# Attention stage: row scores and maxima nearly two heads ahead of the column scores

## The reference, cut to what matters

```
_L1_attn_ref(x, W_qkv, b_qkv, W_out, b_out):      # x: (2, 1024, 512), 16 heads of 32
    q, k, v = split(x @ W_qkv.T + b_qkv)
    scores = einsum('bqhe,bkhe->bhqk', q, k) / sqrt(32)
    scores = where(causal, scores, -inf)
    attn = softmax(scores, axis=-1)
    out = einsum('bhqk,bkhe->bqhe', attn, v)
    out = out.reshape(b, l, 512) @ W_out.T + b_out
```

## Time and profile before

| | |
|---|---|
| median of 3 runs | 1735.79 us (1732.49 to 1737.97) |
| the profiled execution | 1735.57 us |
| its span, first to last instruction | 1733.7 us |
| TensorE clock granted, mean | 0.985 of full |
| busy over the span: PE / DVE / ACT / POOL | 1661.0 / 1018.7 / 655.5 / 557.8 us |
| attention stage within the span | from about 769 to 1157 us |

### The profile page before, as it was taken

The page is one execution under the profiler, slowest core; times in us unless marked ns, Lnnn a source line. Parts: engine busy times, 40 slices in busy tenths (PEclk is TensorE's granted clock), DMA queues, the critical chain, the costliest instruction groups (busy, mean ns, idle before and its releaser), DMA issues. The chain is left out here.

```text
span 1733.7 us, 21900 instructions
## 1 busy us (share of the span) xinstructions
PE 1661.0 (96%) x7804; PEld 1295.1 (75%) x7804; DVE 1018.7 (59%) x1667; ACT 655.5 (38%) x1271; POOL 557.8 (32%) x540
## 2 busy tenths in 40 slices
PE   5999999999999999999989989989999999999998
PEld 3676888788788877876656656658888888888887
DVE  4321365564623454358988989855655555555785
ACT  4421322232213332228878878762222222222221
POOL 4201210310310003117777767672144031033320
PEclk9999999999999999989999999999999999999999
DMA  7200210110101038843554545323010010012243
GB/s 287 102 12 1 61 49 19 55 31 20 60 7 37 25 108 250 291 170 75 121 120 106 122 112 133 79 73 129 0 52 25 1 49 25 1 49 71 76 133 134
DMA packets 101916, 141.80 MB, mean 82 GB/s; under 512 B 43881, under 2 KB 52713, under 8 KB 100274
## 3 DMA queue, kind: packets, MB, share of 16 engines
q1 hardware_dynamic: 100946, 134.05, 26.4%
q10 hardware_dynamic: 864, 6.39, 1.2%
HBM read 93.74 MB, written 46.53 MB: 81 GB/s over the span
## 5 line engine op out<-in xcount | busy, mean ns | idle before, releaser
L1538 ACT ACTIVATE prob<-p_turn 128x512 f32<-128x512 f32 (+3 forms) x384 | 176.2, 487 | 56.9 <-PE p_turn L1510 36.9
L1577 DVE TENSOR_TENSOR pt_lo<-prob,pt_hi 128x512 fp32r<-128x512 f32 (+3 forms) x256 | 173.7, 703 | 33.7 <-ACT pt_hi L1546 33.2
L1570 DVE TENSOR_REDUCE row_top<-p_score 128x1 fp32r<-128x128 f32 (+7 forms) x256 | 184.6, 746 | 14.4 <-PE p_score L1494 12.5
L1025 DVE TENSOR_TENSOR hid<-hid,p_up 128x512 f32<-128x512 f32 x64 | 44.0, 687 | 218.2 <-PE p_up L490 202.5
L1593 POOL TENSOR_TENSOR pt_lo<-prob,pt_hi 128x512 fp32r<-128x512 f32 (+1 forms) x128 | 167.0, 1305 | 10.7
L1924 DVE TENSOR_TENSOR e_hid<-e_hid,e_p_up 128x512 f32<-128x512 f32 x64 | 44.0, 687 | 196.4 <-PE e_p_up L1819 196.4
L1524 PE MATMUL p_o<-pt_hi,v 128*65 128x512 f32 (+3 forms) x384 | 137.9, 362 | 3.9 <-POOL pt_lo L1593 2.3
L1590 POOL TENSOR_SCALAR pt_hi<-prob 128x512 fp32r<-128x512 f32 (+1 forms) x128 | 100.9, 788 | 106.3 <-ACT prob L1538 64.2
L1525 PE MATMUL p_o<-pt_lo,v 128*65 128x512 f32 (+3 forms) x384 | 128.5, 341 | 0.0
L1546 ACT ACTIVATE pt_hi<-prob 128x512 fp32r<-128x512 f32 (+3 forms) x256 | 120.6, 486 | 3.2 <-PE p_o L1525 0.2
L772 ACT ACTIVATE hid<-p_gate 128x512 f32<-128x512 f32 x64 | 38.3, 599 | 218.7 <-PE p_gate L490 218.6
(11 more groups left out here) (279 smaller groups left out, 4256.7 us busy)
## 6 DMA issues: line engine op xcount, KB each, us to landing
stack<-qk_parked SPq DMA_DIRECT2D x66, 256.0 KB, 4.9
raw<-in_wgu SPq DMA_DIRECT2D x64, 256.0 KB, 2.7
qk_parked<-qk SPq DMA_DIRECT2D x16, 1024.0 KB, 4.0
v_parked<-v_out SPq DMA_DIRECT2D x16, 520.0 KB, 7.4
o_parked<-o_both SPq DMA_DIRECT2D x64, 128.0 KB
stack_third<-qk_parked SPq DMA_DIRECT2D x30, 256.0 KB, 4.4
v<-v_parked ACTq DMA_DIRECT2D x6, 1040.0 KB, 8.3
res<-in_x SPq DMA_DIRECT2D x8, 512.0 KB
```

Of the source, the lines that this page charges most:

```text
L1538: act.activation(prob[:, n % PB, c0:W], p_turn[:, n % TB, c0:W], ACT.Exp).then_inc(exped, 1)
L1570: dve.tensor_reduce(top[:, h % 2, r:r + 1], p_score[:, r % 2, 0:width_of(r)], AX_X, ALU.max, negate=True).then_inc(topped, 1)
L1577: dve.tensor_tensor(pt_lo[:, n % PT, c0:W], prob[:, n % PB, c0:W], pt_hi[:, n % PT, c0:W].bitcast(F32), ALU.subtract).then_inc(split, 1)
```

## The change

The lists of all engines except GpSimd are new: rows 1 to 7 are scored and reduced two heads ahead, row 0 (and, on TensorE, row 1) three heads ahead, with `AHEAD` = 3. In the iteration -1 TensorE and VectorE follow a list of their own, `FIRST`. The loads of a pair of heads are issued together at the beginning of each even head, before any place. On ScalarE round 2 moves to the next iteration's start, `read_o` of group 0 comes after exp 4, and round 5 comes after exp 6 where it came before it.

```diff
--- before.py
+++ after.py
@@ -1365,25 +1365,32 @@
     PT = 6
     K3 = 3 * E
     OS = len(o_stored)
-    AHEAD = 2
+    AHEAD = 3
     OWN = (1, 4, 6, 8)
     ORDER = {
-        "tensor": [("weigh", 0, 0), ("weigh", 1, 0), ("score", 5, 1), ("weigh", 2, 0), ("weigh", 3, 0), ("turned", 6, 0),
-                   ("score", 6, 1), ("turned", 7, 0), ("turned", 8, 0), ("weigh", 4, 0), ("weigh", 5, 0), ("score", 7, 1),
-                   ("score", 0, 2), ("turned", 9, 0), ("turned", 10, 0), ("turned", 11, 0), ("weigh", 6, 0),
-                   ("weigh", 7, 0), ("turned", 0, 1), ("score", 1, 2), ("score", 2, 2), ("turned", 1, 1),
-                   ("turned", 2, 1), ("weigh", 8, 0), ("weigh", 9, 0), ("score", 3, 2), ("weigh", 10, 0),
-                   ("weigh", 11, 0), ("score", 4, 2), ("turned", 3, 1), ("turned", 4, 1), ("turned", 5, 1)],
-        "scalar": [("exp", 3, 0), ("exp", 4, 0), ("round", 3, 0), ("exp", 5, 0), ("round", 5, 0), ("read_o", 0, 0),
-                   ("exp", 6, 0), ("exp", 7, 0), ("exp", 8, 0), ("round", 7, 0), ("exp", 9, 0), ("exp", 10, 0),
-                   ("round", 9, 0), ("exp", 11, 0), ("round", 10, 0), ("round", 11, 0), ("exp", 0, 1),
-                   ("round", 0, 1), ("exp", 1, 1), ("exp", 2, 1), ("round", 2, 1), ("read_o", 1, 0)],
-        "vector": [("top", 4, 1), ("rest", 2, 0), ("rest", 3, 0), ("top", 5, 1), ("rest", 5, 0), ("top", 6, 1),
-                   ("rest", 7, 0), ("top", 7, 1), ("top", 0, 2), ("rest", 9, 0), ("top", 1, 2), ("top", 2, 2),
-                   ("rest", 10, 0), ("rest", 11, 0), ("rest", 0, 1), ("top", 3, 2)],
+        "tensor": [("weigh", 0, 0), ("score", 2, 2), ("weigh", 1, 0), ("score", 3, 2), ("weigh", 2, 0), ("weigh", 3, 0),
+                   ("turned", 5, 0), ("turned", 6, 0), ("score", 4, 2), ("turned", 7, 0), ("score", 5, 2), ("turned", 8, 0),
+                   ("weigh", 4, 0), ("turned", 9, 0), ("score", 6, 2), ("turned", 10, 0), ("turned", 11, 0),
+                   ("weigh", 5, 0), ("score", 7, 2), ("weigh", 6, 0), ("turned", 0, 1), ("weigh", 7, 0),
+                   ("turned", 1, 1), ("score", 0, 3), ("weigh", 8, 0), ("weigh", 9, 0), ("weigh", 10, 0),
+                   ("weigh", 11, 0), ("turned", 2, 1), ("turned", 3, 1), ("score", 1, 3), ("turned", 4, 1)],
+        "scalar": [("exp", 3, 0), ("round", 2, 0), ("round", 3, 0), ("exp", 4, 0), ("read_o", 0, 0), ("exp", 5, 0),
+                   ("exp", 6, 0), ("round", 5, 0), ("exp", 7, 0), ("exp", 8, 0), ("round", 7, 0), ("exp", 9, 0),
+                   ("exp", 10, 0), ("round", 9, 0), ("exp", 11, 0), ("round", 10, 0), ("round", 11, 0), ("exp", 0, 1),
+                   ("round", 0, 1), ("exp", 1, 1), ("read_o", 1, 0), ("exp", 2, 1)],
+        "vector": [("top", 1, 2), ("rest", 2, 0), ("rest", 3, 0), ("top", 2, 2), ("top", 3, 2), ("top", 4, 2),
+                   ("top", 5, 2), ("rest", 5, 0), ("top", 6, 2), ("rest", 7, 0), ("rest", 9, 0), ("rest", 10, 0),
+                   ("rest", 11, 0), ("top", 7, 2), ("rest", 0, 1), ("top", 0, 3)],
         "gpsimd": [("divide", 4, 0), ("divide", 6, 0), ("divide", 8, 0), ("divide", 1, 1)],
-        "sync": [("place", 4, 1), ("store", 0, 0), ("place", 5, 1), ("place", 6, 1), ("place", 7, 1),
-                 ("stack", 2, 0), ("place", 0, 2), ("place", 1, 2), ("place", 2, 2), ("place", 3, 2), ("store", 1, 0)],
+        "sync": [("stack", 2, 0), ("place", 1, 2), ("store", 0, 0), ("place", 2, 2), ("place", 3, 2), ("place", 4, 2),
+                 ("place", 5, 2), ("place", 6, 2), ("place", 7, 2), ("store", 1, 0), ("place", 0, 3)],
+    }
+    FIRST = {
+        "tensor": [("score", 2, 2), ("score", 3, 2), ("score", 4, 2), ("turned", 0, 1), ("turned", 1, 1), ("score", 5, 2),
+                   ("turned", 2, 1), ("turned", 3, 1), ("score", 6, 2), ("turned", 4, 1), ("score", 7, 2),
+                   ("score", 0, 3), ("score", 1, 3)],
+        "vector": [("top", 1, 2), ("top", 2, 2), ("top", 3, 2), ("top", 4, 2), ("rest", 0, 1), ("top", 5, 2),
+                   ("top", 6, 2), ("top", 7, 2), ("top", 0, 3)],
     }
 
     with ExitStack() as ctx:
@@ -1439,9 +1446,9 @@
                 else:
                     engine.wait_ge(split, n + 1 - owned(n))
 
-        def run(steps, order):
+        def run(steps, engine):
             for h in range(-AHEAD, HB * QUADS):
-                for step, n, ahead in order:
+                for step, n, ahead in FIRST[engine] if h == -1 and engine in FIRST else ORDER[engine]:
                     if 0 <= h + ahead < HB * QUADS:
                         steps[step](h + ahead, n)
 
@@ -1451,9 +1458,9 @@
         def _(sp):
             def next_stack(h, n):
                 pair = h // 2 + n
-                if pair < HEADS:
+                if h % 2 == 0 and pair < HEADS:
                     wait(sp, turned, 2 * BL * (pair - 2))
-                    load_part(sp, slots[pair % 3], qk_dram, pair, h % 2, stacked[pair % 3])
+                    load_stack(sp, slots[pair % 3], qk_dram, pair, stacked[pair % 3])
                 if h == HB * (QUADS - 1):
                     load_next(sp)
 
@@ -1473,7 +1480,7 @@
                     .then_inc(o_stored[i], 16)
 
             sp.wait_ge(*qk_last)
-            run({"stack": next_stack, "place": place, "store": store}, ORDER["sync"])
+            run({"stack": next_stack, "place": place, "store": store}, "sync")
 
         @block.tensor
         def _(pe):
@@ -1525,7 +1532,7 @@
                 pe.matmul(p_o[0:VC, c0:W], lhs, pt_lo[:, slot, c0:W], start=False,
                           stop=(j in (QB - 1, BL - 1))).then_inc(weighted, 1)
 
-            run({"score": score, "turned": turned_score, "weigh": weigh}, ORDER["tensor"])
+            run({"score": score, "turned": turned_score, "weigh": weigh}, "tensor")
 
         @block.scalar
         def _(act):
@@ -1558,7 +1565,7 @@
 
                     load_values(act, v, v_dram, quad + 1, at // 4, v_loaded[at // 4])
 
-            run({"exp": exp, "round": round_block, "read_o": read_o}, ORDER["scalar"])
+            run({"exp": exp, "round": round_block, "read_o": read_o}, "scalar")
 
         @block.vector
         def _(dve):
@@ -1577,7 +1584,7 @@
                 dve.tensor_tensor(pt_lo[:, n % PT, c0:W], prob[:, n % PB, c0:W], pt_hi[:, n % PT, c0:W].bitcast(F32),
                                   ALU.subtract).then_inc(split, 1)
 
-            run({"top": top_row, "rest": rest}, ORDER["vector"])
+            run({"top": top_row, "rest": rest}, "vector")
 
         @block.gpsimd
         def _(pool):
@@ -1595,7 +1602,7 @@
 
             pool.memset(third[K3:K3 + 1, :, 1].bitcast(F32), 1.0).then_inc(ones_set, 1)
             pool.wait_ge(ones_set, 1)
-            run({"divide": divide}, ORDER["gpsimd"])
+            run({"divide": divide}, "gpsimd")
 
 
 RING = 4
```

## The result

The changed kernel took 1755.8 us (median of 4 runs, 1753.2 to 1763.6), the kernel before 1736.9 beside it: ratio 1.012, 95% interval 1.008 to 1.016. It is slower by 1.2%, clear of the noise. The profiled execution took 1756.79 us with a span of 1754.9, 21.2 longer than before; the forecast was a gain of 14.1.

A forecast was written before the change was run, and what follows sets the result against it. It saw the 387.7 us attention stage bound by heads averaging 11.79 against 10.97 undisturbed, with TensorE waiting for placements. New stage 37.6 + 30 P, P 11.2, gains 14.1: 1735.57 − 14.1 + 0.22 = 1721.7 us, range 1706 to 1744.

The forecast's parts named there:

- The opening: From the first score to the first weigh of head 0: 18.6 us, 5.6 more than before.
- The ending: The last two heads, which have no scores: 9.4 us for head 30 and 9.63 for the last.
- P, the undisturbed head: Time per head of the new order: taken as 11.2 us, bounded by 10.82 and 12.0; no gain at 11.67.
- The rule: A two-input VectorE instruction and a GpSimd instruction reading SBUF exclude each other for the whole instruction, in issue order.
- layout: One head of the new order laid out by hand: 10.82 us without conflicts, 11.76 with them, 11.45 if rest 5 wins.
- The 0.06 us: The lead by which GpSimd's subtraction starts before VectorE's rest 5 is ready, and so holds it.
- port share: Per-head cost of VectorE's rests and GpSimd's subtractions excluding each other: from 10.82 to 11.76 us in the layout.
- The pair loads, costed at 0: Six loads every other head on SP's queue delay nothing due before the next turned scores: 0, at most 11 us.
- The waits of 21.8 us go: TensorE's 21 waits for row_top placements vanish, since the last place is issued some 10.6 us before use, not 4.5.
- The waits stay: Rival, chance 0.08: six loads together make the last place land after 10.6 us; 11 us of gain go, 1732.6.
- port, plain: Rival, chance 0.15: GpSimd's subtraction catches rests 5 and 7 in each head; P 11.5 to 11.8, time 1738.3.
- Port, slower: Rival, chance 0.19: the same meeting, and the next head's rest 0 waits too; P 12.0, loss 9.9, 1745.5 us.

The follow-up runs named there:

- late loads: The changed kernel with the six pair loads moved from before place 1 to behind place 3: 1738.8 us, ratio 0.999.
- the fill: GpSimd's subtraction replaced by a constant fill in the changed kernel: 1744.8 us, ratio 1.003; with the pair loads also behind place 3: 1722.8 us, ratio 0.991.

## Why the prediction was wrong

The time of 1755.8 lies above the range (1744 at the most), and the sign is the other one. Against 1735.57 − 14.1 for the profiled execution the measured one is 35.3 us more: 1.6 before the stage, and 33.8 (rounded) in its terms.

- **The opening**: forecast 18.6, measured 17.7. Right; −0.9. The forecast took the clock at 0.50 from the first score; this execution had 0.94 in the first 2 us (771 to 773). The runs with `FIRST` that start at 0.50, the one with late loads among them, took 18.3, so at the clock it assumed the forecast was 0.3 too high.
- **The ending**: forecast 9.4 + 9.63, measured 10.36 + 10.36: +1.7. That a head without scores is no shorter than 10.36, with `weigh` 8 waiting for GpSimd, was not foreseen.
- **P, the undisturbed head**: I took 11.2, it is 11.65: 30 × 0.45 = +13.5. The rule was in hand and its layout gave 11.76; the failed step is the weighing, "halfway between the measured good head of 10.97 and my 11.45", on the hope that phases settle kindly. The 0.06 us that "decide" fell to GpSimd (0.13 in the trace). That the layout's 11.76 came so near is in part luck: its head without meetings was 10.82, where the fill gives 10.15, and its port share was 0.94, where the fill takes 1.5 away; GpSimd's shorter work counts in both, and the runs do not part it. The waits of weigh 5 and 7 were 0.65 and 0.43, forecast 1.04 and 0.67; some 0.4 of the 1.5 are in no wait that the view lists, and stay open.
- **The pair loads, costed at 0**: they cost 19.5 us over the 30 head starts, and moving them gave 17 back. This is the larger error, and the failed step is the sentence that behind them stands "nothing that is due before the next head's turned scores". The sentence is true, but the places of rows 1 to 3 stand right behind the loads and are due at just that turned 0. I worked out the slack of row 7 (10.6 us), for which no wait is seen, and gave it to all rows. For place 3 the sum was to be: six issues ahead of it (3.3 to 4.1 us, where I had 3.1 by the earlier trace rows), then 9.4 us from its issue to its use, against a landing of 11.6 (8.0 against 12.2 in the head with the weight loads), where I had put 10.0. With the clock behind it a late head cost up to 6.4 us. The upper bound of 11 us charged 0.8 a pair and no slow clock.
- **The waits of 21.8 us go**: in part right. None is at `turned` 4; 13.5 us stand at `turned` 0. "The waits stay" was among the rivals, but at the last place instead of the first ones, with 11 us, and on top of a P that gained.
- **The rivals**: "port, plain" was right for P (11.5 to 11.8) and alone would have given the draw that the late loads measured. "Port, slower" had the sign and was 10 us short, but by a mechanism that did not occur (rest 0 took 0.80, ahead of the subtraction of block 1). I let the two mishaps, port and waits, exclude each other; they came together.

## What to carry to other kernels

Slack has to be worked out for each consumer of a reordered queue, and above all for the group that stands right behind the entry put at its head. A contention rule that the trace bears out goes into the sum at full weight; where hundredths of a microsecond decide it, forecast the costly side. And before work is made shorter, ask what transfers were timed by its length: here most of the 1.5 us off a head came back as waits for placements or loads.

## What the runs showed of the hardware

- A placement of 0.5 KB lands 1.9 us after its issue at the least, 4.9 at the median and 12.2 at the most in the changed kernel (800 to 1150 us); before, 1.9, 4.3 and 8.5. With the six loads behind place 3 it is 1.9, 3.8 and 12.0: what the move changed is which places land late, not how late a single one can be. The Trainium skill, "DMA: Bandwidth & Descriptors", "Queues, rings and completion order", says that each DMA engine takes the descriptors of one ring in order; the late placements behind the loads agree, though no run put the two on different queues.
- A short wait can have a long tail: after 4.24 us of idle TensorE the granted clock was 0.50 for 5.6 us, 6.4 us lost in all; after 2.21 us it was 0.50 again, 4.7 us lost. After 1.34 us it stayed at 1.00, and 1.0 us was lost.
- When a subtraction of GpSimd and a rest of VectorE meet, the one that starts later is stretched, on either side: rest 0.68 to 1.69, subtraction 1.28 to 1.60. A fill by GpSimd across a rest stretched neither (0.52 and 0.68).
